# A longer memset behind GpSimd's indirect DMAs in slots 32 to 61, none outside them, and a small waited one from tile 43

## Chip, cores and metric

One NeuronCore of a Trainium2 chip runs the kernel. The metric is the device time of one execution in microseconds (us); the profile below is of one such execution. TensorE is PE in the profile, VectorE DVE, ScalarE ACT, GpSimd POOL and SyncE SP. "POOL's slot 32" means the pass with s = 32 of a loop that every engine runs through.

## What is computed

The reference takes 8192 rows of 512 floats through a layer with a low-rank term and a GELU, then through a feed-forward net of 16 blocks of which each row uses its four best, and adds the input:

```python
# x: (16, 512, 512), u = v = fside (512 x 16 per batch), b = cond
z = (x @ v / 512) @ u.T / 16
g = gelu(x @ W.T + fc_bias + z + b)              # exact GELU
prob = softmax(g @ w_router + b_router)          # 16 blocks
mask = the 4 largest of prob, per row
h = relu(einsum('nd,ebd->neb', g, w1b) + b1b)    # block width 128
out = x + einsum('neb,ebd,ne->nd', h, w2b, mask) + b2
```

## The kernel before

The 8192 rows come in 16 batches (b) of 512, each of four quarters (q) of 128 rows. A slot s is one quarter of the layer: `layer(s)` on TensorE, `gelu(s)` on ScalarE into the row buffer `grow`, the router, the choice of four blocks (`choose`, `ranks`, `place` on VectorE, once per batch). GpSimd then sends each row of a quarter to the lists of its four blocks in the DRAM buffer `xg`: `place_rows(b, q)` issues four indirect DMAs of 128 rows x 2112 bytes (line 501), in slot s = 4b + q + 7. A row of `grow` may be overwritten two batches later, when those DMAs have landed; `gelu` waits for that (line 590).

A tile j is 512 rows of one block's list (the last 23 tiles are two halves of 256 rows from one or two blocks each; 72 tiles in all, the last one with two chunks). From slot 28 on, each slot also has a tile of the feed-forward net: SyncE loads tile j (`load_tile`, line 333) once the rows that it can hold are placed and the table that names its block and position is written (`place_tiles`, lines 513 and 518), TensorE turns it (`turn_tile`), multiplies (`ffn1`, `ffn2`), ScalarE and VectorE split operands into a high and a low part and take chunks 0 and 2 (ScalarE, line 668) and 1 and 3 (VectorE, line 952) of the result to `ys`, `stx` or `grow`. GpSimd sends the four chunks to `yt` in DRAM, to the rows' places, in slot j + 30: `send(j, c)`, line 528. The result buffers are two until tile 36, then three to five; whoever takes a result waits until the buffer's former tile has been sent.

After the tiles, `yt` is read back in order, the four results of a row are summed with x and the bias on VectorE, and written out.

The layer ends with slot 63, the placing with slot 70, the tiles with slot 99. In slots 31 to 66 GpSimd sends a tile's results first and places rows after; before and after it is the other way about.

After each indirect DMA of `place_rows` and `send` GpSimd calls `rest()` (line 487): it waits until the memset before has ended and writes 16 floats per partition of `pace`, which nobody reads. The DMAs of `place_tiles` have no memset behind them.

Of the kernel before, what the change touches and what calls it, by code (L numbers as in the profile page):

```python
# [9 lines left out]
NE = 16  # L10
# [8 lines left out]
SLOTS = 4 * NB  # L19
LAG = 28  # L20
# [12 lines left out]
MORE = 39, 43, 55  # L33
EARLY = 12
AHEAD = EARLY + 8

ALU = mybir.AluOpType
ACT = mybir.ActivationFunctionType
AX = mybir.AxisListType
F32 = mybir.dt.float32  # L40
# [13 lines left out]
def chunks(j):  # L54

    return 2 if j == NTILE - 1 and HALVES % 2 == 1 else 4
# [17 lines left out]
def row_buffer(b):  # L74

    return b % 3 if b < 6 else b % 2
# [26 lines left out]
def result_buffer(j):  # L103
    return RESULT_BUFFER[j]
# [57 lines left out]
def adaln_ffn(nc, xT, xrow, fvT, fuT, cond, fc, wT, wrT, br, w1T, b1T, w2T, b2R, outT):  # L162
    with ExitStack() as ctx:
        def sb(name, shape, dt):
            return ctx.enter_context(nc.sbuf_tensor(name, shape, dt))

        def sem(name):
            return ctx.enter_context(nc.semaphore(name))
# [10 lines left out]
        w2l = sb("w2l", [P, NE, D], F32R)  # L179
# [99 lines left out]
        g_z, g_id, g_up, g_tok, g_k, g_s, g_pace = (  # L279
            sem(n) for n in ("g_z", "g_id", "g_up", "g_tok", "g_k", "g_s", "g_pace"))  # L280
# [165 lines left out]
        @block.gpsimd  # L446
        def _(pool):
            pool.memset(idf[:, :], 0.0).then_inc(g_z, 1)
            pool.memset(upper[:, :], 0.0).then_inc(g_z, 1)
            pool.memset(base[:, :], 0.0).then_inc(g_z, 1)  # L450
            pool.memset(tzero[:, :, 0:2], 0).then_inc(g_z, 1)
            pool.memset(tzero[:, :, 2:4], HALF).then_inc(g_z, 1)
            pool.wait_ge(g_z, 5)
            pool.affine_select(out=idf[:, :], in_=idf[:, :], compare_op=ALU.not_equal, fill=1.0, base=0,
                               pattern=[[-1, P]], channel_multiplier=1).then_inc(g_id, 1)
            pool.affine_select(out=upper[:, :], in_=upper[:, :], compare_op=ALU.is_ge, fill=1.0, base=0,
                               pattern=[[-1, P]], channel_multiplier=1).then_inc(g_up, 1)
            for p, each, first in ((0, LRING, 0), (32, HALF, HALF), (64, 0, 1)):
                pool.wait_ge(g_up, 1 + p // 32)
                pool.iota(base[p:p + 1, :], [[each, NE]], base=first, channel_multiplier=0,  # L460
                          allow_small_or_imprecise_dtypes=True).then_inc(g_up, 1)
            pool.wait_ge(g_up, 4)
            pool.iota(tokid[:, :], [[TOPK * P, SLOTS]], base=0, channel_multiplier=TOPK).then_inc(g_tok, 1)
            pool.iota(thr[:, :], [[TILE, NE]], base=TILE, channel_multiplier=0,
                      allow_small_or_imprecise_dtypes=True).then_inc(g_k, 1)
            pool.iota(spare[:, :], [[0, 1]], base=96, channel_multiplier=1,
                      allow_small_or_imprecise_dtypes=True).then_inc(g_k, 1)
            pool.iota(ebase[:, :], [[0, 1]], base=HALF, channel_multiplier=LREG,
                      allow_small_or_imprecise_dtypes=True).then_inc(g_k, 1)
            pool.iota(tval[:, :, 0], [[0, 2]], base=0, channel_multiplier=1).then_inc(g_k, 1)  # L470
            pool.memset(tval[:, :, 1:4], 0).then_inc(g_k, 1)
            pool.iota(twice[:, :], [[0, 1]], base=2 * 96, channel_multiplier=2,
                      allow_small_or_imprecise_dtypes=True).then_inc(g_k, 1)
            pool.iota(hoff[:, :], [[HALF, 2]], base=0, channel_multiplier=0,
                      allow_small_or_imprecise_dtypes=True).then_inc(g_k, 1)
            pool.iota(lim[:, :], [[LREG, NE]], base=LREG, channel_multiplier=0,
                      allow_small_or_imprecise_dtypes=True).then_inc(g_k, 1)
            pool.iota(order[:, :], [[1, 2]], base=0, channel_multiplier=2).then_inc(g_k, 1)
            pool.memset(sumk[:, :], 0.0).then_inc(g_s, 1)
            for k in range(KC):  # L480
                pool.wait_ge(g_s, k + 1)
                pool.affine_select(out=sumk[:, :], in_=sumk[:, :], compare_op=ALU.not_equal, fill=1.0, base=-2 * NE * k,
                                   pattern=[[-1, NE]], channel_multiplier=1).then_inc(g_s, 1)

            paced = [0]

            def rest():

                if paced[0] > 0:
                    pool.wait_ge(g_pace, paced[0])  # L490
                pool.memset(pace[:, :], 0.0).then_inc(g_pace, 1)  # L491
                paced[0] += 1

            def place_rows(b, q):
                pool.wait_ge(v_ix, b + 1)
                j = 4 * (b - RING + 3) - 1
                if j >= 0:
                    pool.wait_ge(s_gr[j % 2], 32 * (j // 2 + 1))
                    pool.wait_ge(s_gr[1 - j % 2], 32 * ((j - 1) // 2 + 1))
                for k in range(TOPK):  # L500
                    pool.indirect_dma_start(  # L501
                        out=xg, out_offset=bass.IndirectOffsetOnAxis(ap=ix[:, row_buffer(b), q, k:k + 1], axis=0),
                        in_=grows[row_buffer(b)][:, q, :], in_offset=None).then_inc(s_sc[row_buffer(b)][q], 16)
                    rest()

            def place_tiles(n):
                pool.wait_ge(v_tb, n + 1)
                if n == 0:
                    pool.wait_ge(s_t0, 16)
                else:  # L510
                    pool.wait_ge(s_tb, 16 * n)
                if n < NB:
                    pool.indirect_dma_start(out=table, out_offset=bass.IndirectOffsetOnAxis(ap=tpos[:, 0:1], axis=0),
                                            in_=tval[:, :, :].rearrange("e h f -> e (h f)"),
                                            in_offset=None).then_inc(s_tb, 16)
                    return
                for h in range(2):
                    pool.indirect_dma_start(out=table.rearrange("r (h f) -> (r h) f", h=2),
                                            out_offset=bass.IndirectOffsetOnAxis(ap=thalf[:, h:h + 1], axis=0),
                                            in_=tval[:, h, :], in_offset=None).then_inc(s_tb, 16)  # L520

            def send(j, c):

                if c % 2 == 0:
                    pool.wait_ge(a_y, 2 * j + c // 2 + 1)
                else:
                    pool.wait_ge(v_y, 2 * j + c // 2 + 1)
                pool.indirect_dma_start(  # L528
                    out=yt, out_offset=bass.IndirectOffsetOnAxis(ap=ids[:, j % 8, c:c + 1], axis=0),
                    in_=yss[result_buffer(j)][:, c, :], in_offset=None, bounds_check=ROWS * TOPK - 1,  # L530
                    oob_is_err=False).then_inc(s_y[result_buffer(j)], 16)
                rest()

            for s in range(LAG + NTILE + 2):
                b, q = divmod(s, 4)
                j = s - LAG - 2
                first = s <= LAG + 2 or SLOTS + 3 <= s
                if 0 <= s - 7 < SLOTS and first:
                    place_rows((s - 7) // 4, (s - 7) % 4)
                if 0 <= j < NTILE:  # L540
                    for c in range(chunks(j)):
                        send(j, c)
                if 0 <= s - 7 < SLOTS and not first:
                    place_rows((s - 7) // 4, (s - 7) % 4)
                if q == 0 and 2 <= b <= NB:
                    place_tiles(b - 2)
                if s == 4 * (NB + 1) + 1:
                    place_tiles(NB - 1)
                if s == 4 * (NB + 1) + 4:
                    place_tiles(NB)  # L550
# [178 lines left out]
        def _(dve):  # L729
# [192 lines left out]
            def presplit_w2(e):  # L922

                dve.wait_ge(p_w, SLOTS)
                dve.wait_ge(a_p2, e + 1)
                dve.tensor_tensor(w2l[:, e, :], w2f[:, e, :], w2h[:, e, :].bitcast(F32), ALU.subtract).then_inc(v_p2, 1)

            def split_w2(j, e):
# [81 lines left out]
            for s in range(LAG + NTILE + 1):  # L1010
                b, q = divmod(s, 4)
                j = s - LAG
# [54 lines left out]
                if SLOTS + 19 <= s < SLOTS + 19 + EARLY:  # L1067
                    with_bias(s - SLOTS - 19)
            for i in range(EARLY, AHEAD):
                with_bias(i)  # L1070
            for i in range(NSUM - 1):
                total(i)
                if i + AHEAD < NSUM:
                    with_bias(i + AHEAD)
            for h in range(2):
# [244 lines left out]
```

## Time and profile before

| | us |
|---|---|
| median of 3 runs (1112.36 to 1116.27) | 1112.42 |
| the profiled execution | 1113.2 |
| its span | 1111.1 |
| PE busy | 853.7 |
| DVE busy | 826.8 |
| POOL busy | 645.5 |
| ACT busy | 579.1 |

The span is what the trace covers; all positions are us from its start. Around it lie 2.1 us of the execution's own time. A line of a timeline has the start, the length, the engine, the kernel's line, the operation, what it writes and reads, and in brackets the idle time ahead of it with what ended that. "issue" stands for idle time in which the engine waited for nothing that the profile shows. The row of an indirect DMA on POOL is the engine's part in it, not the transfer, which ends some us later ("landing"). Memsets stand at L491.

### The profile page before, as it was taken

To read this page: it belongs to the slowest core of one execution; us is meant where nothing else is said; L and a number is where in the kernel's file an instruction comes from. 1 tells how busy PE (TensorE), PEld (TensorE's weight loads), DVE (VectorE), ACT (ScalarE), POOL (GpSimd) and SP (SyncE) were. 2 spreads that over 40 slices of the span, in tenths; PEclk is the share of its full clock that TensorE was granted. 3 is DMA by queue.
4 is the path that set the end of the run, shared out by engine and by line. 5 is a ranking of instruction groups with operands and counts; after the bars stand their busy time and mean duration, and the time that the engine had idled before them with its cause. 6 is when DMAs were issued, how large, how long until landed. Compare 5 with 4: busy or idle time off the path is not lost.

```text
span 1111.1 us, 18547 instructions
## 1 busy us (share of the span) xinstructions
PE 853.7 (77%) x4924; PEld 680.6 (61%) x4924; DVE 826.8 (74%) x1964; ACT 579.1 (52%) x1061; POOL 645.5 (58%) x1131
## 2 busy tenths in 40 slices
PE   8999969999999999999999888999999900000000
PEld 7777747777787777778777666888888800000000
DVE  4566547777767767776767897788989779878787
ACT  6555537576676667667567676667767600000000
POOL 1488886777777787777778887656555630000000
PEclk9999989999999999999999999999999965555555
DMA  6799788898989899899879888889887689999999
GB/s 194 235 372 332 265 296 302 293 324 301 310 308 319 305 299 318 313 308 308 303 269 319 336 293 320 282 296 319 287 304 247 211 345 415 425 429 430 428 429 386
DMA packets 103238, 354.85 MB, mean 319 GB/s; under 512 B 29961, under 2 KB 29961, under 8 KB 92384
## 3 DMA queue, kind: packets, MB, share of 16 engines
q1 hardware_dynamic: 59104, 217.21, 56.2%
q0 software_dynamic: 43936, 136.37, 31.2%
q8 instruction: 41, 0.67, 0.3%
q14 instruction: 61, 0.50, 0.1%
q10 hardware_dynamic: 96, 0.10, 0.0%
HBM read 200.47 MB, written 169.65 MB: 333 GB/s over the span
## 4 chain that ended last, share of the span: by engine, by line
PE 51%; DMA 18%; POOL 9%; DVE 6%; SPq 6%; issue 5%; ACT 3%; ACTq 1%; POOLq 0%; DVEq 0%
PE lay L1105 12%; DMA w2l<-yt 11%; PE yps L1244 10%; PE hid L1213 9%; PE trn L1198 6%; POOL xg L501 6%; PE hid L1218 4%; SPq L342 4%; DMA tabi<-table 3%; PE trn L1126 2%; DVE stx L968 2%; PE hid L1091 2%; POOL yt L528 2%; DMA outT<-ys 2%; PE rps L1141 1%
## 5 line engine op out<-in xcount | busy, mean ns | idle before, releaser
L528 POOL DMA_INDIRECT yt<-ys,ids x218 | 229.3, 1052 | 121.7 <-ACT ys L668 76.5
L501 POOL DMA_INDIRECT xg<-grow,ix x224 | 224.1, 1000 | 80.8 <-DVE ix L851 42.5
L777 DVE TENSOR_TENSOR gsb<-trn,gsb 128x512 fp32r<-128x512 f32 x241 | 162.3, 687 | 116.1 <-ACT gsb L609 115.4
L1105 PE MATMUL lay<-w2l,xs 128*128 128x512 f32 x768 | 190.1, 397 | 0.0
L1105 PEld LDWEIGHTS lay<-w2l,xs 128*128 128x128 f32 x768 | 141.9, 189 | 29.3
L1198 PE MATMUL trn<-idf,gr 128*128 128x128 f32 x964 | 148.8, 279 | 13.6 <-DMA tabi<-table 11.0
L609 ACT ACTIVATE gsb<-trn 128x512 fp32r<-128x512 f32 x241 | 143.5, 596 | 22.6 <-PE trn L1198 22.0
L1198 PEld LDWEIGHTS trn<-idf,gr 128*128 128x128 f32 x964 | 118.5, 143 | 50.4 <-DVE gsb L777 12.8
L1213 PE MATMUL hid<-gsb,w1c 128*128 128x512 f32 (+1 forms) x576 | 128.0, 364 | 0.0
L1244 PE MATMUL yps<-w2c,hh 128*128 128x512 f32 x340 | 122.4, 442 | 5.4 <-issue 4.7
L637 ACT ACTIVATE hv<-hid,b1c 128x512 f32<-128x512 f32 (+1 forms) x94 | 52.6, 584 | 134.1 <-PE hid L1218 133.2
L1213 PEld LDWEIGHTS hid<-gsb,w1c 128*128 128x128 f32 x576 | 95.2, 188 | 16.5 <-ACT gsb L609 0.4
L491 POOL MEMSET pace<- 128x16 f32 x542 | 75.6, 140 | 0.1
L592 ACT ACTIVATE grow<-lay 128x512 f32<-128x512 f32 x56 | 33.5, 598 | 71.5 <-PE lay L1110 49.2
L1244 PE MATMUL yps<-w2c,hl 128*128 128x512 f32 x170 | 68.0, 400 | 0.0
L1218 PE MATMUL hid<-gsb,w1c 128*128 128x512 f32 (+1 forms) x288 | 67.6, 357 | 0.0
L952 DVE COPY ys<-yps 128x512 f32<-128x512 f32 x93 | 63.1, 681 | 1.2 <-DMA xg<-ys,ix 1.2
L668 ACT ACTIVATE ys<-yps 128x512 f32<-128x512 f32 x99 | 59.2, 598 | 3.6 <-PE yps L1244 1.7
L1244 PEld LDWEIGHTS yps<-w2c,hh 128*128 128x128 f32 x340 | 51.7, 192 | 7.9 <-issue 5.6
L528 POOL DMA_INDIRECT yt<-stx,ids x40 | 41.5, 1038 | 25.0 <-ACT stx L668 14.6
L1218 PEld LDWEIGHTS hid<-gsb,w1c 128*128 128x128 f32 x288 | 49.5, 189 | 8.1
L968 DVE TENSOR_TENSOR stx<-xs 128x1024 f32<-128x1024 f32 x32 | 37.8, 1221 | 22.0 <-DMA xs<-yt 22.0
(205 smaller groups left out, 1688.1 us busy)
## 6 DMA issues: line engine op xcount, KB each, us to landing
gr<-xg SPq DMA_DIRECT2D x49, 1056.0 KB
xs<-yt SPq DMA_DIRECT2D x16, 2048.0 KB, 19.5
w2l<-yt SPq DMA_DIRECT2D x15, 2048.0 KB, 19.7
gr<-xg SPq DMA_DIRECT2D x45, 528.0 KB
stx<-xT SPq DMA_DIRECT2D x64, 256.0 KB, 3.6
outT<-ys SPq DMA_DIRECT2D x31, 512.0 KB, 20.4
xg<-xrow SPq DMA_DIRECT2D x16, 528.0 KB, 6.6
w2f<-xrow SPq DMA_DIRECT2D x16, 512.0 KB, 13.5
```

The costliest lines, as they stand in the source:

```text
L491: pool.memset(pace[:, :], 0.0).then_inc(g_pace, 1)
L501: pool.indirect_dma_start(out=xg, out_offset=bass.IndirectOffsetOnAxis(ap=ix[:, row_buffer(b), q, k:k + 1], axis=0), in_=grows[row_buffer( ...
L528: pool.indirect_dma_start(out=yt, out_offset=bass.IndirectOffsetOnAxis(ap=ids[:, j % 8, c:c + 1], axis=0), in_=yss[result_buffer(j)][:, c, ...
L609: act.activation(gsb[:, :, HI, c * P:(c + 1) * P], turned[TURN_BANK[n]][:, :].rearrange("p (k t) -> p k t", k=KC), ACT.Copy).then_inc(a_tn, 1)
L777: dve.tensor_tensor(gsb[:, :, LO, c * P:(c + 1) * P], turned[TURN_BANK[n]][:, :].rearrange("p (k t) -> p k t", k=KC), gsb[:, :, HI, c * P: ...
L952: dve.tensor_copy(yss[result_buffer(j)][:, c, :], second_out[RESULT_BANK[4 * j + c]][:, :]).then_inc(v_y, 1)
L968: dve.tensor_tensor(two[:, 2 * h:2 * h + 2, :], y[:, 4 * h:4 * h + 2, :], y[:, 4 * h + 2:4 * h + 4, :], ALU.add).then_inc(v_k, 1)
L1105: pe.matmul(lay[s % 2][:, :], xs[:, b % 2, k, h, cols], wls[:, k, a, :], start=(k == 0 and a == HI and h == HI), stop=False)
L1198: last = pe.transpose(turned[TURN_BANK[n]][:, k * P:(k + 1) * P], gr[:, j % 2, c, k * P:(k + 1) * P], idf[:, :])
L1213: pe.matmul(hid[:, cols], w1x[h][:, a, k * P:(k + 1) * P], gsb[:, k, HI, cols], start=(h == 0 and k == 0 and a == HI), stop=False)
L1218: last = pe.matmul(hid[:, cols], w1x[h][:, HI, k * P:(k + 1) * P], gsb[:, k, LO, cols], start=False, stop=(h == len(parts) - 1 and k == KC ...
L1244: last = pe.matmul(second_out[RESULT_BANK[n]][:, :], hx[:, c * P:(c + 1) * P], w[a], start=(i == 0), stop=(i == 2))
```

## The change

`rest()` now writes 256 floats per partition, into a part of `w2l` that is free until the last block's second weights are split there, and is called only in slots 32 to 61 (30 slots with four row DMAs and four result DMAs each, 240 calls). Outside them no memset stands behind an indirect DMA, except for tiles from 43 on: behind the tile's second result GpSimd calls `stop()`, which writes 16 floats and waits for its own memset. VectorE waits for the 240 memsets before it writes the last block of `w2l`.

```diff
+PACE_FROM = LAG + 4
+PACE_TO = SLOTS - 2
+REST = 256
...
                 if paced[0] > 0:
                     pool.wait_ge(g_pace, paced[0])
+                pool.memset(w2l[:, NE - 1, 0:REST].bitcast(F32), 0.0).then_inc(g_pace, 1)
+                paced[0] += 1
+
+            def stop():
+
                 pool.memset(pace[:, :], 0.0).then_inc(g_pace, 1)
                 paced[0] += 1
-
-            def place_rows(b, q):
+                pool.wait_ge(g_pace, paced[0])
+
+            def place_rows(b, q, paced_now):
...
-                    rest()
+                    if paced_now:
+                        rest()
...
-            def send(j, c):
+            def send(j, c, paced_now):
...
-                rest()
+                if paced_now:
+                    rest()
+                elif j >= SLOTS + 7 - LAG and c == 1:
+                    stop()
...
-                    place_rows((s - 7) // 4, (s - 7) % 4)
+                    place_rows((s - 7) // 4, (s - 7) % 4, PACE_FROM <= s < PACE_TO)
...
-                        send(j, c)
+                        send(j, c, PACE_FROM <= s < PACE_TO)
...
                 dve.wait_ge(a_p2, e + 1)
+                if e == NE - 1:
+                    dve.wait_ge(g_pace, 8 * (PACE_TO - PACE_FROM))
                 dve.tensor_tensor(w2l[:, e, :], w2f[:, e, :], w2h[:, e, :].bitcast(F32), ALU.subtract).then_inc(v_p2, 1)
```

## Rows read from the trace of the kernel before

**Rows 1.** The chain that ended last: shares of the span by engine.

```profile
PE 51%; DMA 18%; POOL 9%; DVE 6%; SPq 6%; issue 5%; ACT 3%; ACTq 1%; POOLq 0%; DVEq 0%
```

**Rows 2.** Stretch, its length, busy us of each engine, clock, DMA share, GB/s.

```profile
81.20:152.00 70.80, 63.61 (x365) 46.61 (x364) 39.76 (x174) 37.20 (x65) 60.63 (x106) 0.95 0.85 302
200.60:562.50 361.90, 361.70 (x2015) 284.55 (x2012) 263.94 (x742) 241.27 (x439) 278.80 (x488) 1.00 0.90 309
598.00:664.90 66.90, 60.17 (x310) 46.47 (x309) 59.36 (x163) 47.30 (x86) 57.71 (x99) 0.97 0.85 314
690.00:884.00 194.00, 186.30 (x1232) 162.22 (x1231) 163.11 (x347) 133.35 (x264) 113.62 (x194) 1.00 0.81 275
```

**Rows 3.** Timeline of POOL, 622 to 627 us.

```profile
622.65 0.12 POOL L491 MEMSET pace<- 128x16 f32 x1
622.95 0.97 POOL L501 DMA_INDIRECT xg<-grow,ix  x1 [0.18 <-issue]
...
625.49 1.00 POOL L528 DMA_INDIRECT yt<-ys,ids  x1 [0.18 <-issue]
626.46 0.16 POOL L491 MEMSET pace<- 128x16 f32 x1
626.80 1.00 POOL L528 DMA_INDIRECT yt<-ys,ids  x1 [0.18 <-issue]
```

**Rows 4.** The chain that ended last, 596 to 700 us.

```profile
658.30 2.97 DMA xg<-grow,ix
662.07 6.79 DMA tabi<-table
```

**Rows 5.** POOL's groups, 200.6 to 562.5 us: busy, mean ns, idle before.

```profile
L528 POOL DMA_INDIRECT yt<-ys,ids x120 | 123.1, 1026 | 57.6 <-ACT ys L668 36.0 <-issue 19.7 <-DMA tabi<-table 1.9
L501 POOL DMA_INDIRECT xg<-grow,ix x120 | 118.6, 988 | 24.5 <-issue 20.2 <-DVE ix L851 4.3
L491 POOL MEMSET pace<- 128x16 f32 x240 | 33.7, 141 | 0.0
L513 POOL DMA_INDIRECT table<-tval,tpos x8 | 6.8, 854 | 1.4 <-issue 1.4
```

**Rows 6.** Timeline of POOL: DMAs that follow a table DMA without a memset.

```profile
653.49 0.97 POOL L501 DMA_INDIRECT xg<-grow,ix  x1 [0.30 <-issue]
...
678.73 0.90 POOL L518 DMA_INDIRECT table<-tval,thalf  x1 [0.30 <-issue]
679.93 1.01 POOL L528 DMA_INDIRECT yt<-grow,ids  x1 [0.30 <-issue]
```

**Rows 7.** POOL's memsets: groups, two rows of the timeline, and line 491's durations.

```profile
L448 POOL MEMSET idf<- 128x128 f32 x1 | 0.2, 204 | 0.3 <-POOLq L1313 0.3
L479 POOL MEMSET sumk<- 128x16 f32 x1 | 0.1, 101 | 0.0
...
0.74 0.20 POOL L448 MEMSET idf<- 128x128 f32 x1 [0.29 <-POOLq L1313]
0.88 0.20 POOL L449 MEMSET upper<- 128x128 bf16 x1
...
L491 POOL MEMSET pace<- x542: 125/142/167, 43.5 to 899.0; 128x16 f32 x181
```

**Rows 8.** Waits, 200.6 to 562.5 us: who for whom, total, times, longest.

```profile
ACT hv L637 <- PE hid L1218: 56.3, 30, 2.6
...
ACT grow L592 <- DMA xg<-grow,ix: 22.1, 10, 3.5
```

**Rows 9.** Waits of POOL, 562.5 to 599.4 us.

```profile
POOL yt L528 <- ACT ys L668: 3.9, 5, 0.9
POOL yt L528 <- issue: 2.0, 8, 0.6
```

**Rows 10.** Timeline of POOL at its end.

```profile
870.91 1.28 POOL L528 DMA_INDIRECT yt<-stx,ids  x1 [0.74 <-DVE stx L952]
...
884.01 0.98 POOL L528 DMA_INDIRECT yt<-ys,ids  x1 [1.26 <-ACT ys L668]
```

## What the change does to the time: the prediction

> **What bounds the kernel now.** I read the chain that ended last first, then a table of engines by stage, then GpSimd (POOL) alone. The chain is half TensorE, and POOL has 9% of it [rows 1]. The table tells where [rows 2]. From 200.6 to 562.5 us TensorE is busy for 361.7 of 361.9 us: this is POOL's slots 32 to 61, 12.06 us each, and nothing but TensorE sets the pace. In two other stretches POOL is nearly closed: 81 to 152 us (60.6 busy of 70.8, and the rest are the 0.18 us gaps that follow its instructions) and 598 to 665 us (57.7 of 66.9). In both the chain runs through POOL's row scatters at L501, one every 1.27 to 1.28 us: 0.97 DMA, 0.12 or 0.13 memset, 0.18 gap; [rows 3] has the second stretch, and the first repeats it 60 times. The second stretch ends when the last rows land at 661.3 (2.97 us from 658.30) and the next tile's load takes another 6.8 us [rows 4]; all later tiles wait for that. From 690 to 884 TensorE is 96% busy again and POOL 59%. After 900 us only the sums and their DMAs run, which POOL doesn't touch.
>
> **What POOL needs in slots 32 to 61.** The 240 DMAs, their 240 memsets and 8 table DMAs are busy for 123.1 + 118.6 + 33.7 + 6.8 = 282.2 us [rows 5]. To them come 240 gaps of 0.18 behind memsets and 8 of 0.30 behind table DMAs (rows of both kinds in [rows 3] and [rows 6]): 43.2 + 2.4. A result DMA's row overlaps its memset by 0.03 (626.46 against 625.49 + 1.00), 120 times: 3.6 less. Need: 324.2 us of 361.9. So POOL has 37.7 us to spare, **0.157 us for each of the 240 DMAs**. It sits in the two waits of a tile's first sends for ACT and DVE.
>
> **Part 1: the memset grows from 16 to 256 floats, 240 times.** The trace has 128x16 at 101 ns and 128x128 at 204 ns, both early in the kernel where POOL is alone [rows 7]: 0.92 ns per further element. 240 elements more are 0.22 us. No 256-wide memset is in the trace, so I bound it. Upper end: the fixed part were nothing and 256 cost twice 204, 0.41 less today's 0.14, so +0.27. Lower end: the two 128x128 memsets start 0.14 us apart in the trace (their rows overlap), so 256 might occupy only 0.28: +0.14. I take 0.22, the slope between two rows of the same operation. Is the 0.18 behind it still paid? Memsets of 0.12 to 0.16 us are all followed by 0.18 [rows 3], so the gap adds to the memset and doesn't absorb it.
> The Trainium skill (GPSIMD Engine Reference, section 3.1, Elementwise) gives a port-bound 1.03 cycles per element for simple bodies; at its 1.2 GHz that would be an estimated 0.206 us, and a lag of 49.4 - 37.7 = 11.7 us in place of the 15.1 below. The same skill (SBUF — State Buffer, section Who interferes with whom) says that a VectorE instruction with two SBUF inputs holds up a GpSimd instruction that reads SBUF, not one that only writes. By that rule memsets aren't stretched by VectorE, however long they are; the trace agrees, 125 to 167 ns over all 542.
> 240 x 0.22 = 52.8 us against 37.7 to spare: POOL becomes the bound at 12.57 us a slot against 12.06, and ends slot 61 **15.1 us late** (ends: 33.6 - 37.7, no lag; 64.8 - 37.7 = 27.1).
>
> **What the lag runs into.** Behind POOL stand a tile's result DMAs, on which ACT and DVE wait for a free result buffer, and the rows of slot s - 7, on which the GELU two batches later and the tile loads wait. The nearest limit is the GELU: ACT already waits for row DMAs 10 times, 22.1 us, and what hides it is ACT's own wait for TensorE ahead of the hidden layer, 56.3 us in 30 slots, 1.9 each [rows 8]. So after some 2 to 3 us of lag TensorE is held back too and then runs at POOL's rate. That doesn't stop the lag in absolute time; it only means that TensorE is late with POOL.
>
> **Part 2: no memset in the other slots.** Behind a DMA with no memset the next starts 0.30 us after it, wherever its data are ready: ten times behind table DMAs, one of them a pair of table DMAs back to back [rows 6]; with one it is 0.13 + 0.18 = 0.31. So removing the small memset saves 0.01 us per DMA, not 0.31: 60 DMAs in the first POOL stretch, -0.6 us; 72 from slot 62 to 70, -0.7. These are the only places where POOL's rate counts. The gap's lower bound is nothing, which is a rival below.
>
> **Where the lag ends.** From slot 62 POOL has its old need again but little slack: until 599 us it is idle 3.9 + 2.0 us ahead of 13 result DMAs [rows 9]; less 13 x 0.18 that stays and 0.57 of the first, which is counted above, 3.0 us. From 598 it never waits. So 15.1 - 3.0 = 12.1 us of lag arrive at the last row scatter, and by [rows 4] move everything behind it.
>
> **Part 3: the small memset with a wait, from tile 43.** Third sends start later. A DMA that waited for another engine's result starts with 0.74 us idle ahead of it, against 0.18 in line [rows 10]: about +0.6 us per tile. From 690 to 884 POOL is 41% idle [rows 2] and has three to five result buffers, so this costs nothing. In the last 13 us the sends of tiles 69, 70 and 71 stand in line (from 884.01, ten DMAs): two stops lie inside, +1.2 us on the path (bounds 0.2 to 1.4; if DMA landings of the second send were quicker for it, I would not see it here). VectorE's new wait for the 240th memset is met in slot 61, and its presplit runs from slot 66: nothing. The 240 writes go to w2l's last expert block, read by nobody then.
>
> **Sum.** 15.1 - 3.0 - 0.6 - 0.7 + 1.2 = +12.0 us on the profiled execution's 1113.2, 1125.2; the median of the runs is 0.8 lower, so **1124 us**. Own range: L of 10 to 27 us, 1119 to 1136; the upper end holds also a dearer case, in which the rows' landing (POOL waits for a result that waits for its own rows) adds some tenths of a us per slot.
>
> **Rivals.**
> (a) The longer memset is hidden, wholly or down to +0.14. For: the gap behind a bare DMA (0.30) almost equals memset plus gap (0.31), as if the next DMA's start were due at 0.30 whatever lies between. Against: the 0.18 didn't shrink when the memset was 0.16. It decides at 0.157 us per DMA: below that POOL stays inside 12.06 us a slot and TensorE sets the pace. Time: 1113.2 - 0.6 - 0.7 + 1.2 - 0.8 = 1112. The Trainium skill (Perfetto Trace Analysis, section DMA Instruction — SWDGE (GPSIMD)) has the row of such a DMA end when the last descriptor is written, ahead of the end of its execution. By that rule the 0.30 could be the DMA's own tail, and a memset could run beneath it.
> (b) Not slower: without a memset the row DMAs follow more closely than 0.30 us, down to some 0.06. The place is 81 to 152 and 598 to 665 us. It would save up to 0.24 x 60 and 0.24 x 44, but TensorE is busy for 63.6 of 70.8 and 60.2 of 66.9 us there [rows 2], so it takes over after 7.2 and 6.7 us. Off the sum: 1124 - 13.9 = 1110, no measurable change. It outweighs the lag from a gap of about 0.18 on; together with (a) it gives 1098, clearly faster. For it speaks only that no two row DMAs stand back to back in the trace; against it, all ten gaps are 0.30, also where a row or a result DMA follows.
> (c) The change doesn't do what it says: the pace is no pace and the DMAs only move among themselves; that is (a) with 1112.
>
> **How the numbers follow.** Chances: forecast 0.58 (1119 to 1136), (a) and (c) 0.14, (b) alone 0.12, (a) and (b) together 0.11, other mechanisms 0.05. This kernel's measurement tells 0.5% (5.6 us) from no change. Slower by more than that: 0.58; within: 0.24; faster: 0.18. The range goes from the near edge of the fast case to the dear end of the forecast, 1100 to 1135.
>
> **What would show it.** In the profile after: memset rows of 0.34 to 0.38 us at L494 or its like; POOL without waits for ACT from some slot after 32 on, and its slots at 12.5 us; TensorE's share in 200 to 575 us down from 100% to 96%, with ACT's GELU waiting for row DMAs; the last row scatter near 670 in place of 658. Bare row DMAs 1.27 us apart in the first stretch confirm part 2; 1.0 to 1.1 apart would be (b). Memset rows of 0.35 but slots still at 12.06 would be (a). The third send of late tiles some 0.7 us later, and the last landing 1 us later than the lag alone says, confirm part 3. The forecast falls if the memset costs under 0.157 us more, or if a gap that I take as fixed isn't.

## The result

| | before | changed |
|---|---|---|
| median of 4 runs | 1114.13 us (1112.36 to 1116.27) | 1124.74 us (1123.01 to 1126.33) |
| the profiled execution | 1113.2 | 1123.69 |
| its span | 1111.1 | 1121.9 |

The changed kernel takes 1.0098 times as long, with a 95% interval of 1.0075 to 1.0121; a second measurement gave 1.0097 (1.0072 to 1.0122). The forecast was 1124 us. The median before is of four runs here; the 1112.42 us from which the forecast started was of the first three.

Where the time lies is read from five points of the timeline of POOL. They cut the execution into stretches; each is given in us, from one profiled execution of each kernel (a send is the indirect DMA of one result chunk):

| stretch | before | changed |
|---|---|---|
| start to the first send of slot 32 | 200.7 | 203.1 |
| slots 32 to 61 | 362.3 | 372.9 |
| slot 62 to the last row scatter | 95.4 | 92.5 |
| to the first send of tile 43 | 21.6 | 21.4 |
| tile 43 to the last send | 217.1 | 218.1 |
| to the end | 214.0 | 214.0 |

The stretch of the long memsets grew by 10.6 us and the next one shrank by 2.9. Another 2.4 us of the difference lie ahead of slot 32, where no long memset runs; they are taken up below.

The page of the changed kernel: busy time and share of the span per engine, the chain that ended last by engine, and the group of the long memset (count, busy us, mean ns, idle before).

```profile
PE 857.7 (76%) x4924; PEld 682.2 (61%) x4924; DVE 827.6 (74%) x1964; ACT 577.8 (52%) x1061; POOL 669.1 (60%) x858
PE 32%; POOL 24%; DMA 19%; issue 12%; DVE 6%; ACT 6%; ACTq 1%; SPq 0%; POOLq 0%; DVEq 0%
L494 POOL MEMSET w2l<- 128x256 f32 x240 | 82.0, 342 | 0.0
```

POOL's part of the chain went from 9% [rows 1] to 24%, TensorE's from 51% to 32%. The same lines of POOL in slots 32 to 61 as in [rows 5], now over 203 to 575.9 us:

```profile
L538 POOL DMA_INDIRECT yt<-ys,ids x120 | 123.4, 1029 | 22.0 <-issue 19.7 <-ACT ys L681 1.4 <-DVE ys L967 0.5
L510 POOL DMA_INDIRECT xg<-grow,ix x120 | 121.1, 1009 | 19.7 <-issue 19.6 <-ACT ys L681 0.2
L494 POOL MEMSET w2l<- 128x256 f32 x240 | 82.0, 342 | 0.0
L523 POOL DMA_INDIRECT table<-tval,tpos x8 | 7.6, 947 | 1.3 <-issue 1.1 <-DVE ys L967 0.2
```

The idle time ahead of the result DMAs fell from 57.6 us, of which 36.0 were waits for ACT, to 22.0, of which 1.4 are: POOL hardly waits for another engine any more. Three lines of its timeline, with the start, the length and the idle time ahead, show the new step, 1.46 us from start to start:

```profile
408.56 0.97 POOL L510 DMA_INDIRECT xg<-grow,ix  x1 [0.17 <-issue]
409.52 0.34 POOL L494 MEMSET w2l<- 128x256 f32 x1
410.02 0.97 POOL L510 DMA_INDIRECT xg<-grow,ix  x1 [0.17 <-issue]
```

Who waits for POOL is in the waits of the same stretch (total, times, longest), to be read beside [rows 8]:

```profile
ACT grow L605 <- DMA xg<-grow,ix: 67.1, 22, 6.0
ACT hv L650 <- PE hid L1233: 32.2, 20, 2.6
```

and TensorE's busy time in it, the sum row of the table of [rows 2], asked for PE alone:

```profile
sum 372.90, PE 367.45; mean PE 367.45
```

The GELU waited 22.1 us for row DMAs and now waits 67.1. ACT's wait for TensorE, which hid that, shrank from 56.3 to 32.2 us, and TensorE itself is now open for 5.5 us where it was open for 0.2. That is only half of the 10.6 us: TensorE ran 2038 matmuls in these slots of POOL where it had run 2015, so it got 5.75 us of busy time further ahead of POOL before it was held back.

### The profile page after: what moved, and what is told of

Same layout as the page of the kernel before. It is cut to its first block, busy times and chain, and to the rows that moved or that the text cites. A ratio compares the mean times of both kernels' runs of the same rounds, so it can differ in the third digit from the quotient of the medians.

```text
span 1121.9 us, 18303 instructions
## 1 busy us (share of the span) xinstructions
PE 857.7 (76%) x4924; PEld 682.2 (61%) x4924; DVE 827.6 (74%) x1964; ACT 577.8 (52%) x1061; POOL 669.1 (60%) x858
## 4 chain that ended last, share of the span: by engine, by line
PE 32%; POOL 24%; DMA 19%; issue 12%; DVE 6%; ACT 6%; ACTq 1%; SPq 0%; POOLq 0%; DVEq 0%
POOL xg L510 13%; DMA w2l<-yt 11%; PE hid L1228 8%; PE yps L1259 7%; POOL yt L538 6%; PE lay L1120 5%; PE hid L1233 4%; PE trn L1213 4%; POOL w2l L494 3%; DMA tabi<-table 3%; DVE stx L983 2%; DMA xg<-grow,ix 2%; ACT gsb L622 2%; DMA outT<-ys 2%; PE lay L1259 1%
## 5 line engine op out<-in xcount | busy, mean ns | idle before, releaser
L538 POOL DMA_INDIRECT yt<-ys,ids x218 | 232.6, 1067 | 87.8 <-issue 39.2
L494 POOL MEMSET w2l<- 128x256 f32 x240 | 82.0, 342 | 0.0
L538 POOL DMA_INDIRECT yt<-stx,ids x40 | 45.7, 1142 | 28.0 <-ACT stx L681 8.7
L983 DVE TENSOR_TENSOR stx<-xs 128x1024 f32<-128x1024 f32 x32 | 37.7, 1221 | 25.3 <-DMA xs<-yt 25.3
## 6 DMA issues: line engine op xcount, KB each, us to landing
w2f<-xrow SPq DMA_DIRECT2D x16, 512.0 KB, 13.3
```

What stands on the lines that cost most here:

```text
L494: pool.memset(w2l[:, NE - 1, 0:REST].bitcast(F32), 0.0).then_inc(g_pace, 1)
L538: pool.indirect_dma_start(out=yt, out_offset=bass.IndirectOffsetOnAxis(ap=ids[:, j % 8, c:c + 1], axis=0), in_=yss[result_buffer(j)][:, c, ...
L983: dve.tensor_tensor(two[:, 2 * h:2 * h + 2, :], y[:, 4 * h:4 * h + 2, :], y[:, 4 * h + 2:4 * h + 4, :], ALU.add).then_inc(v_k, 1)
```

## The experiments

The theory: in slots 32 to 61 the longer memset uses up the 0.157 us that POOL had to spare per DMA; what it takes beyond that arrives, less what the next stretch absorbs, at the end. The rivals: the small memsets that were removed outside those slots are the cost (they had kept row DMAs from bunching ahead of tile loads), or a bare DMA follows faster, or the stop costs more than its own length.

Each run was timed in several rounds beside the kernel before on the same chip; a ratio is against that, with a 95% interval.

### The size back at 16 floats

```diff
-REST = 256
+REST = 16
```

> The changed kernel with the memset of slots 32 to 61 back at 16 floats; all else as changed. Theory (GpSimd's rate in slots 32 to 61 is the cost): the lag is gone, 1112 to 1116 us, slot 61 ends near 565 us. Rival (the missing memsets outside these slots, or the stop, are the cost): it stays near 1124.

1117.72 us (1117.62 to 1117.90), ratio 1.0035 (1.0019 to 1.0051). Slots 32 to 61 took 362.1 us, so the lag is gone with the size. The time is above the 1112 to 1116 that was expected: 3.7 us over before remain, of which the stop is one suspect (below).

### The long memset alone

The kernel before with this edit in its `rest()`, in slots 32 to 61 only; outside them the 16 floats as before, no stop. VectorE's wait for the long memsets is kept, as it is in all kernels below except the two without any memset:

```diff
-                pool.memset(pace[:, :], 0.0).then_inc(g_pace, 1)
+                pool.memset(w2l[:, NE - 1, 0:REST].bitcast(F32), 0.0).then_inc(g_pace, 1)
```

> The kernel before with the 256-float memset in slots 32 to 61 and nothing else changed: 16-float memsets outside, no stop. Theory: the whole loss, 1121 to 1125 us. Rival (missing memsets or stop): 1112 to 1115.

1123.13 us, 1.0095 (1.0077 to 1.0113). Slots 32 to 61 took 373.7 us. So part 1 alone brings about a loss of this size, and the removed memsets are not needed for it. The interval overlaps that of the changed kernel (1.0075 to 1.0121), so it leaves room for a few us of the other parts.

### No stop

```diff
                 if paced_now:
                     rest()
-                elif j >= SLOTS + 7 - LAG and c == 1:
-                    stop()
```

> The changed kernel without the waited memset from tile 43 on. Theory: about 1 us less than changed, 1123 to 1125, the last send 1 us earlier. Rival (the stop delays late tiles or their loads): 3 us or more less.

1120.66 us, 1.0066 (1.0043 to 1.0088): 4.1 us less than changed by the medians, not 1. The intervals of the two overlap, so this is only a first hint that part 3 was priced too low.

### No memset and no stop anywhere

```diff
-                    if paced_now:
-                        rest()
...
-                if paced_now:
-                    rest()
-                elif j >= SLOTS + 7 - LAG and c == 1:
-                    stop()
```

> No memset behind any indirect DMA and no stop. Theory: DMAs 1.27 us apart, as with the 16-float memset, so 1111 to 1115 us. Rival (a memset spaces the DMAs and a bare one follows closely): 1100 to 1108. Rival (the memsets kept DMAs from bunching ahead of tile loads): 1118 or more.

1113.34 us, 1.0003 (0.9990 to 1.0017). The timeline of POOL, in the first stretch that it bounds:

```profile
109.75 0.96 POOL L510 DMA_INDIRECT xg<-ys,ix  x1 [0.30 <-issue]
111.01 0.96 POOL L510 DMA_INDIRECT xg<-grow,ix  x1 [0.31 <-issue]
112.28 1.39 POOL L510 DMA_INDIRECT xg<-grow,ix  x1 [0.30 <-issue]
```

Bare DMAs start 1.26 to 1.27 us apart, as with a 16-float memset between them. The rival of the closely following DMA is refuted. So is the one that the small memsets did something for the time, to within the interval of 0.17%.

### Bare only before slot 32, and bare only from slot 62

In the profiles of the first four runs slot 32 began 2.4 to 4.3 us late where the early memsets were missing. Two kernels looked for that; each is the kernel before with this condition at its two calls of `rest()` (the second with `s < PACE_TO`):

```diff
-                    rest()
+                    if s >= PACE_FROM:
+                        rest()
```

> The kernel before with no memset in slots before 32, all else as before. By the traces of the first four runs slot 32 comes 2.4 to 4.3 us later without them: theory that this is caused by the missing memsets: +2 to +4 us, 1115 to 1118. Rival (a whim of single executions, or tied to the other parts): 1112 to 1114, slot 32 at 200.7.

> The kernel before with no memset from slot 62 on, all else as before. Theory from the stretch between the last scatter and the last send (238.8 before, 237.0 and 234.9 without memset or stop): 2 to 3 us faster, 1110 to 1112. Rival (the gain needs the lag): same as before, 1113 to 1114.

1112.62 us, 0.9984 (0.9966 to 1.0002), and 1113.14 us, 0.9990 (0.9976 to 1.0004). Neither differs from before, and both forecasts of a change missed. Whether the late start of slot 32 is scatter is not settled by the profiles. For scatter: the second kernel's code is that of before up to slot 61, yet its slot 32 began at 202.2 in place of 200.7, and the first row scatter, which no edit precedes, starts anywhere from 42.0 to 44.7 us. Against it: slot 32 began at 202.7 to 205.0 in all eleven profiles without the early memsets and at 200.5 to 202.2 in the three with them; counted from the first row scatter it is 159.1 to 161.5 us against 158.5 to 160.2. What the ten runs of the first kernel show is that it costs nothing in the total. Executions of one kernel mostly spread over 5 to 9 us here, and a stretch of one profile is worth no more than that allows.

### 128 floats and 512 floats

The diff is that of the first of two kernels; the second has 512.

```diff
-REST = 256
+REST = 128
```

> The changed kernel with 128 floats in place of 256. A memset would take 0.24 us, about 0.10 more than the 16-float one, less 0.01 of the gap: under the 0.157 us to spare, so no lag. Theory: as with 16 floats, 1117 to 1119 us, slots 32 to 61 in 362 us. Rival (every added us of POOL counts, since its slack is not where it is needed): halfway, 1120 to 1122.

> The changed kernel with 512 floats. The step from 16 to 256 was 0.201 us, so 512 is about 0.21 more: 240 x 0.21 = 51 us more in slots 32 to 61, all of it lag. Theory: 1172 to 1178 us, slots 32 to 61 in about 424 us. Rival (other terms grow with the lag, or the tail absorbs more of it): outside that.

1113.63 us, 0.9992 (0.9972 to 1.0011), and 1172.79 us, 1.0514 (1.0489 to 1.0538). The memset's durations (min/median/max in ns) of the two and of the 16-float kernel, in this order, from their views of the line:

```profile
L494 POOL MEMSET w2l<- x240: 218/236/263, 204.2 to 565.3; 128x128 f32 x120
```

```profile
L494 POOL MEMSET w2l<- x240: 538/556/588, 205.9 to 629.7; 128x512 f32 x120
```

```profile
L494 POOL MEMSET w2l<- x240: 125/141/169, 206.0 to 566.3; 128x16 f32 x120
```

| floats | memset, ns | slots 32 to 61, us |
|---|---|---|
| 16 | 141 | 362.1 |
| 128 | 236 | 362.5 |
| 256 | 341 | 372.4 to 374.0 (six kernels) |
| 512 | 556 | 425.5 |

The 512-float kernel came as forecast. The 128-float kernel kept its slots at 362.5 us as forecast; its time lay below the 1117 to 1119 expected, which stays open (see the end of the next part). This is the bend that the theory wants. 0.095 us more per DMA cost nothing, under the 0.157 to spare; 0.200 cost 11.1 us (mean 373.3 less the 362.2 of the kernels without lag); beyond it every further us is paid in full: (425.5 - 372.9) / 240 = 0.219 against 0.215 by the rows. The 128-float kernel keeps a good part of its waits for ACT, 13.3 us of 36.0:

```profile
L538 POOL DMA_INDIRECT yt<-ys,ids x120 | 127.1, 1059 | 34.7 <-issue 20.1 <-ACT ys L681 13.3 <-DMA tabi<-table 1.3
```

### With and without the stop, once more

The changed kernel as it is, and without the stop (the edit shown above), on one chip:

> The changed kernel once more, beside the next one on the same chip. Theory: 10 to 11 us over before (1124 to 1125). Its tail, from VectorE's bias adds at L973 to the last send: about 8 us, as in its first trace (899.85 to 907.90).

> The changed kernel without the stop, once more. Theory (the stop pushes two more sends under the bias adds, where one lasts 1.97 us in place of 0.98): 3.4 us less than changed, the tail 4.6 us. Rival (the 4 us between the two in the first runs were scatter): within 1 us of changed.

1127.10 us, 1.0097 (1.0072 to 1.0122), against 1122.76, 1.0068 (1.0042 to 1.0093): 4.3 us by the medians, after 4.1, but 3.2 by the ratios, and the intervals overlap again. The last sends of the first trace of the changed kernel, POOL's timeline and then VectorE's:

```profile
897.54 0.99 POOL L538 DMA_INDIRECT yt<-stx,ids  x1 [0.30 <-issue]
898.84 0.98 POOL L538 DMA_INDIRECT yt<-stx,ids  x1 [0.30 <-issue]
899.79 0.16 POOL L499 MEMSET pace<- 128x16 f32 x1
901.02 2.04 POOL L538 DMA_INDIRECT yt<-stx,ids  x1 [1.07 <-issue]
903.36 1.97 POOL L538 DMA_INDIRECT yt<-stx,ids  x1 [0.30 <-issue]
905.63 1.97 POOL L538 DMA_INDIRECT yt<-ys,ids  x1 [0.30 <-issue]
907.90 1.96 POOL L538 DMA_INDIRECT yt<-ys,ids  x1 [0.30 <-issue]
```

```profile
899.85 4.62 DVE L973 TENSOR_TENSOR gr<-gr,fu 128x1024 f32<-128x1024 f32 x4
904.39 4.63 DVE L973 TENSOR_TENSOR w1f<-w1f,fu 128x1024 f32<-128x1024 f32 x4
```

those of the kernel without the stop, in the second measurement:

```profile
903.52 0.98 POOL L538 DMA_INDIRECT yt<-stx,ids  x1 [0.30 <-issue]
904.81 0.98 POOL L538 DMA_INDIRECT yt<-stx,ids  x1 [0.31 <-ACT ys L679]
906.10 1.11 POOL L538 DMA_INDIRECT yt<-stx,ids  x1 [0.30 <-issue]
907.51 1.97 POOL L538 DMA_INDIRECT yt<-ys,ids  x1 [0.30 <-issue]
909.78 1.97 POOL L538 DMA_INDIRECT yt<-ys,ids  x1 [0.30 <-issue]
```

```profile
905.13 4.62 DVE L971 TENSOR_TENSOR gr<-gr,fu 128x1024 f32<-128x1024 f32 x4
909.67 4.62 DVE L971 TENSOR_TENSOR w1f<-w1f,fu 128x1024 f32<-128x1024 f32 x4
```

and the last two sends of the kernel before, whose adds start at 892.42:

```profile
894.79 1.97 POOL L528 DMA_INDIRECT yt<-ys,ids  x1 [0.18 <-issue]
897.06 1.97 POOL L528 DMA_INDIRECT yt<-ys,ids  x1 [0.18 <-issue]
```

When VectorE has taken the last result, it adds the bias to eight parts of x (L973, eight adds of 128x1024). A send beside them lasts 1.97 us and not 0.98. From the adds' start to the last send's it is 907.90 - 899.85 = 8.05 us with the stop and 909.78 - 905.13 = 4.65 without: the stop makes POOL later against VectorE, and two more sends fall under the adds. Its price in the tail is 3.4 us. The other profiles repeat it: 4.65 us in all seven profiles without the stop in which the adds are not held back, 8.05 or 8.06 in four with it, and 7.0 in the 16-float kernel, where three sends are long. From the last send to the end it is 213.8 to 214.7 us in all of these. The total agrees with the price, but doesn't prove it: from tile 43's first send to the adds it takes 208.3 to 213.2 us without the stop and 208.4 to 210.7 with it, so a part that the stop gives back earlier isn't excluded.

### The bias adds held back

If the adds are what stretches the sends, they must not start ahead of the last one. The first line stands behind GpSimd's last send:

```diff
+            pool.memset(pace[:, 0:1], 0.0).then_inc(g_last, 1)
...
+            dve.wait_ge(g_last, 1)
             for i in range(EARLY, AHEAD):
                 with_bias(i)
```

> The changed kernel, but VectorE holds the last 8 bias adds back until GpSimd has issued the last send. Theory of the tail: no send lasts 1.97 us any more, so 4 us less of sends; the adds (9.2 us) then still end about when the first parts of the sum land. 1120 to 1122. Rival (long sends come from something else): still 1.97 us each, 1124 or more.

> No memset and no stop anywhere, with the adds held back as in the one before. Theory: the two last sends are 0.98 in place of 1.97 us, so 2 us under the kernel without memsets (1113.3): 1111 to 1112, the fastest of all here. Rival (the held adds come onto the path): 1113 or more.

The first, the changed kernel with this edit: 1123.15 us, 1.0072 (1.0057 to 1.0087), 4.0 under the changed kernel of the same chip. Its last sends, and VectorE's adds behind them:

```profile
899.93 0.98 POOL L538 DMA_INDIRECT yt<-stx,ids  x1 [1.07 <-issue]
901.22 0.98 POOL L538 DMA_INDIRECT yt<-stx,ids  x1 [0.30 <-issue]
902.51 0.98 POOL L538 DMA_INDIRECT yt<-ys,ids  x1 [0.30 <-issue]
903.80 0.98 POOL L538 DMA_INDIRECT yt<-ys,ids  x1 [0.30 <-issue]
```

```profile
905.10 4.63 DVE L974 TENSOR_TENSOR gr<-gr,fu 128x1024 f32<-128x1024 f32 x4 [6.25 <-POOL pace L564]
```

All four are 0.98 us. That settles the cause of the long sends in the tail. The gain of 4.0 us is as forecast, though the intervals of the two overlap; the time itself lay above the 1120 to 1122 that was expected, as that of the changed kernel did on this chip.

The second, no memset or stop and the adds held back: 1114.12 us, 0.9988 (0.9975 to 1.0001). Its last sends are all 0.99 us, but the 2 us don't show beyond the scatter; it is no proven improvement over before. The time fits the rival (1113 or more), but the profile doesn't: from the last send to the end it is 213.9 us, no longer than before. No kernel here beats before measurably.

## Why the prediction was right

**The total** of 1124 against 1124.74 is better than its terms were, and that closeness is luck. The lag was forecast 4.0 us too high. Against it, what the next stretch absorbs was put 1.4 too high, the stop 2.2 too low, and the 0.6 us for the early memsets don't show; this nearly cancels. The starting time was 1.7 us too low as well (the median of before was to rise to 1114.13), which made up for a forecast change of 12.0 us against a measured one of 10.6.

**Part 1, POOL as the bound:** the mechanism is shown from both sides, by the size taken back, by the long memset alone and by the bend between 128 and 256 floats. The lag, forecast 15.1 us, measured 11.1 (mean of six kernels; 10.6 in the changed kernel's profile, worked out here). The term was sized too high in two places. A memset is 0.201 us longer (342 less 141 ns), not 0.22: between 128 and 512 floats it is 0.83 ns an element, not the 0.92 that two lone memsets at the start gave. That is 4.5 us over 240. And the gap behind the longer memset is 0.165, not 0.18: another 3.6, which the DMAs' own growth, 123.4 + 121.1 + 7.6 = 252.1 us busy against 248.5, takes back. 48.3 - 3.6 + 3.6 - 37.7 = 10.6. The lower end of the range (+0.14, rows that overlap) was wrong as a price: the whole row counted. The estimate from the Trainium skill's element rate (GPSIMD Engine Reference, section 3.1), 0.206 us and a lag of 11.7, was nearer than mine. Its rule on who blocks whom (SBUF — State Buffer, section Who interferes with whom) agrees with the trace for memsets: the 256-float ones are 325 to 371 ns over all 240, none stretched like the last sends.

**What the lag runs into:** GELU waits, ACT's slack shrinking and TensorE losing only what is left came as described. But TensorE was to be held back after 2 to 3 us of lag, and it took about 5: it lost 5.3 us of the 10.6, and its share fell to 98.5%, where I had said 96%. The total doesn't hang on this, since the stretch behind it ends with POOL's row scatters.

**Where the lag ends:** I took off 3.0 us of slack and 0.7 for the memsets. Together that is 3.7, and it was 1.4 too much: the stretch shrank by 2.3 us in the mean of the six kernels with 256 floats (93.0 against 95.3 of the seven with none, 16 or 128).

**Part 2, no memset elsewhere:** right. The gap of 0.30 us read behind table DMAs holds behind every bare DMA, and three kernels show no effect on the time. (From 81.2 to 152 us the trace of before has 52 row scatters, not 60; the 0.6 us would be 0.5.) Rival (b) is refuted by the 1.26 us steps. Rival (a) is refuted by the changed kernel's 1.46 us steps. Rival (c) held for the small memsets, which space nothing, and fell for the long ones.

**Part 3, the stop:** the term that was sized too low, 1.2 against 3.4 us in the tail. I priced only the stop's own delay. The step that failed is that I counted the ten last sends at a constant length, though the last two of before already lasted 1.97 us. I hadn't asked what stood beside them; a later send isn't only later, it falls under the bias adds and doubles.

**The sum by measured terms** is 11.1 - 2.3 + 3.4 = 12.2 us against 10.6 measured (10.8 in the spans). This sum leaves out the 2.4 us ahead of slot 32. The difference is within what executions of one kernel spread.

**What stays open:** the kernel with 16 floats and the stop is 3.7 us over before, the one with 128 floats and the stop 0.6 under its own before. Both have the stop, and long sends are in both profiles, four with 128 floats and three with 16. The five runs of the 16-float kernel lie within 0.3 us, where most kernels spread over 5 to 9, so its interval may be too narrow. The stretches of the profiles show no cause for the difference, and it wasn't pursued. So the stop's 3.4 us are shown in the tail; in the total the two pairs with 256 floats point the same way, and the 128-float kernel doesn't.

## What to carry to other kernels

An engine that idles a little in every slot has a budget per instruction: add up its busy time and its unavoidable gaps over the stage, and divide what is left by the number of places where the edit adds something. Here an edit below that was free (0.095 us of 0.157), and above it each further nanosecond counted in full. And before a late instruction is moved by a microsecond, look at what runs on its neighbours at the new place: it may last twice as long there.

## What the hardware showed that I had not expected

- An indirect DMA of 128 rows mostly lasts 0.98 us, and 1.97 us while VectorE runs back-to-back adds of 128x1024 floats with both inputs in SBUF; with the adds moved away the last four are 0.98 again.
- A 16-float memset between two indirect DMAs is free: 0.97 + 0.13 + 0.18 with it, 0.96 + 0.30 without.
- A GpSimd memset takes 141, 236, 341 and 556 ns for 16, 128, 256 and 512 floats per partition behind an indirect DMA.
- After a wait for its own memset GpSimd's next indirect DMA starts 0.78 to 1.07 us after that memset's end, where it starts 0.30 behind a DMA in line.
